# Grouped feed-forward: order of shared and routed blocks, of the routing's products, and of the weight remainders

## What is computed (the reference, cut)

```python
scores = softmax(x @ gate_w.T)                       # 16 experts
topk_w, topk_idx = top_k(scores, 4); topk_w /= sum(topk_w)
for each expert e:  y += w_e * ((silu(x @ wg_e.T) * (x @ wu_e.T)) @ wd_e.T)     # I = 176
y += (silu(x @ sg.T) * (x @ su.T)) @ sd.T            # shared, I = 352
x = x + y
```

## Time and profile before

| | |
|---|---|
| median of 3 runs | 1520.65 us (1513.06 to 1520.93) |
| the profiled execution | 1517.63 us, span 1515.8 us, mean granted TensorE clock 0.936 |
| TensorE matmul busy | 1306.7 us (86%) |
| VectorE, ScalarE, POOL busy | 1032.8, 852.6, 865.5 us (68, 56, 57%) |
| chain that ended last | PE 40%, issue 20%, POOL 18%, DVE 12%, DMA 5%, ACT 3% |
| gathers, L1041 | 94, mean 1060 ns |
| scatters, L1050 | 94, mean 1012 ns |
| raw weight loads | 36 of 608 KB |

### The profile page before, as it was taken

The page is one execution under the profiler, slowest core; times in us unless marked ns, Lnnn a source line. Parts: engine busy times, 40 slices in busy tenths (PEclk is TensorE's granted clock), DMA queues, the critical chain, the costliest instruction groups (busy, mean ns, idle before and its releaser), DMA issues.

```text
span 1515.8 us, 28468 instructions
## 1 busy us (share of the span) xinstructions
PE 1306.7 (86%) x8066; PEld 1100.9 (73%) x8066; DVE 1032.8 (68%) x2536; ACT 852.6 (56%) x2102; POOL 865.5 (57%) x760
## 2 busy tenths in 40 slices
PE   5999999999777993759899999899999989768983
PEld 3888888888767883537777777677777769667872
DVE  5676666657547544438888888788888867547544
ACT  1444444454326542238787877687787866226542
POOL 3555555531335774257877777778687721235772
PEclk8999999999869997769999999999999999779996
DMA  3000000002325336121222222222222202326335
GB/s 114 26 26 26 26 25 25 16 27 67 108 85 174 113 102 226 40 57 34 65 58 70 60 57 54 57 55 56 57 53 50 50 16 75 122 71 195 102 103 180
DMA packets 52271, 110.72 MB, mean 73 GB/s; under 512 B 11616, under 2 KB 21408, under 8 KB 51872
## 3 DMA queue, kind: packets, MB, share of 16 engines
q1 hardware_dynamic: 40992, 82.22, 18.9%
q0 software_dynamic: 9024, 24.65, 5.5%
q10 hardware_dynamic: 2112, 2.10, 0.4%
HBM read 64.11 MB, written 15.47 MB: 52 GB/s over the span
## 4 chain that ended last, share of the span: by engine, by line
PE 40%; issue 20%; POOL 18%; DVE 12%; DMA 5%; ACT 3%; POOLq 0%; SPq 0%; DVEq 0%; ACTq 0%
PE ps L1463 26%; PE ps L1618 7%; POOL pb_odd L1102 4%; POOL yt L1102 3%; DMA raw_w<-in_wx 3%; POOL rb L1087 2%; PE ps L1826 2%; POOL z L1102 2%; DVE rb L545 2%; DVE x_res L855 2%; POOL ra L1091 1%; POOL pb_low L1102 1%; DMA xg<-zbuf,gidx 1%; PE ps L1716 1%; PE ps L1550 1%
## 5 line engine op out<-in xcount | busy, mean ns | idle before, releaser
L914 DVE TENSOR_TENSOR pt_lo<-ps,pt_hi 128x512 fp32r<-128x512 f32 (+3 forms) x384 | 205.3, 549 | 52.4 <-ACT pt_hi L1382 46.2
L1463 PE MATMUL ps<-kh,qh 128*128 128x512 f32 (+3 forms) x768 | 203.1, 374 | 20.9 <-DMA qh<-qt_hi 9.0
L1382 ACT CAST pt_hi<-ps 128x512 fp32r<-128x512 f32 (+3 forms) x384 | 178.8, 482 | 56.4 <-PE ps L1826 48.5
L899 DVE TENSOR_REDUCE nmb<-ps 128x1 f32<-128x1024 f32 (+7 forms) x256 | 191.9, 750 | 27.1 <-PE ps L1463 26.0
L1463 PEld LDWEIGHTS ps<-kh,qh 128*128 128x128 f32 x768 | 131.2, 195 | 44.1 <-issue 12.8
L1463 PE MATMUL ps<-pt_hi,vst 128*128 128x512 f32 (+3 forms) x384 | 155.8, 406 | 1.6 <-DVE ra L879 1.6
L1041 POOL DMA_INDIRECT xg<-zbuf,gidx x94 | 99.6, 1060 | 58.4 <-PE ps L1688 23.0
L1463 PE MATMUL ps<-pt_lo,vst 128*128 128x512 f32 (+3 forms) x384 | 132.2, 348 | 0.0
L1179 ACT ACTIVATE pa<-sma,nmax 128x192 f32<-128x192 f32 x128 | 57.3, 449 | 129.4 <-DVE nmax L582 105.2
L1006 POOL TENSOR_TENSOR pa<-pa,rinv 128x384 f32<-128x384 f32 x64 | 52.9, 827 | 130.6 <-DVE rinv L590 130.6
L1463 PE MATMUL ps<-w_ex,gx_hi 128*128 x376 | 102.4, 355 | 18.6 <-issue 17.7
(11 more groups left out here) (223 smaller groups left out, 4206.8 us busy)
## 6 DMA issues: line engine op xcount, KB each, us to landing
raw_w<-in_wx SPq DMA_DIRECT2D x36, 608.0 KB
rb<-raw SPq DMA_DIRECT2D x192, 64.0 KB, 2.0
yg<-ybuf SPq DMA_DIRECT2D x8, 1024.0 KB, 8.0
qh<-qt_hi SPq DMA_DIRECT2D x64, 128.0 KB, 2.3
qh<-qt_lo SPq DMA_DIRECT2D x64, 128.0 KB, 2.4
wa<-in_wa SPq DMA_DIRECT2D x16, 384.0 KB, 3.0
wb<-in_wb SPq DMA_DIRECT2D x8, 384.0 KB, 3.3
wo_a<-in_wo_a SPq DMA_DIRECT2D x16, 128.0 KB, 2.0
```

Of the source, the lines that this page charges most:

```text
L899: v.tensor_reduce(nmb[:, par, i:i + 1], ps[:, b:b + 2, :].rearrange("p b k -> p (b k)")[:, 0:P * (t + 1)], AX.X, ALU.max, negate=True).the ...
L914: v.tensor_tensor(pt_lo[:, s % 3, at], ps[:, 4 + s % 2, at], pt_hi[:, s % 3, at].bitcast(F32), ALU.subtract).then_inc(sem("b_pt_lo"), 1)
L1382: s_.copy(pt_hi[:, s % 3, at], ps[:, 4 + s % 2, at]).then_inc(sem("b_pt_hi"), 1)
L1463: return t_.matmul(o, l, r, start=start, stop=stop)
```

## The change

- `ORDER`: ten shared blocks, then three times two routed and two shared ones, then the remaining routed blocks. Before: twelve, and twice two and two.
- The second logits move from step 4 to 3, the ranks from 5 to 4, and both halves of the table stand in step 7.
- VectorE: `tables` stands ahead of `experts`; `shifted` comes one step later; in the first stage the remainder of attention b's value weights moves from behind the last step into the last but one.
- ScalarE: the exponential moves behind the last block's output.
- POOL takes the remainders of weights 0 to 5 only; VectorE takes 6 and 7 too. The steps of all copies and remainders are new.

```diff
--- before.py
+++ after.py
@@ -51,12 +51,14 @@
 NBP = 48
 NSH = NT * N_SH
 NM = NSH + NB
-FRONT = 12
-ORDER = ([("s", n) for n in range(FRONT)] + [("r", 0), ("r", 1), ("s", 12), ("s", 13), ("r", 2), ("r", 3), ("s", 14), ("s", 15)] +
-         [("r", b) for b in range(4, NB)])
+FRONT = 10
+ORDER = [("s", n) for n in range(FRONT)]
+for u in range((NSH - FRONT) // 2):
+    ORDER += [("r", 2 * u), ("r", 2 * u + 1), ("s", FRONT + 2 * u), ("s", FRONT + 2 * u + 1)]
+ORDER += [("r", b) for b in range(NSH - FRONT, NB)]
 AT = {item: j for j, item in enumerate(ORDER)}
 N_W = N_SH + NE
-POOL_LO = 8
+POOL_LO = 6
 XG_RING = 4
 YB_RING = 4
 TILE_ROWS = TOPK * P + TOPK
@@ -829,15 +831,16 @@
                 step(5)
                 hot(1)
                 step(6)
+                tables()
                 experts()
-                tables()
+                step(7)
                 shifted()
-                for j in range(7, NM):
+                for j in range(8, NM):
                     step(j)
-                if s == "f":
-                    dve.wait_ge(sem("b_wv_hi"), 1)
-                    v.tensor_tensor(wvb_lo[:, :, :], wvb[:, :, :], wvb_hi[:, :, :].bitcast(F32),
-                                    ALU.subtract).then_inc(sem("b_wv_lo"), 1)
+                    if s == "f" and j == NM - 2:
+                        dve.wait_ge(sem("b_wv_hi"), 1)
+                        v.tensor_tensor(wvb_lo[:, :, :], wvb[:, :, :], wvb_hi[:, :, :].bitcast(F32),
+                                        ALU.subtract).then_inc(sem("b_wv_lo"), 1)
                 dve.wait_ge(sem(f"{s}_ex"), since(s, "ex") + 1)
                 link(v.tensor_reduce(csum[:, :], ex[:, :, :], AX.X, ALU.add))
                 link(v.reciprocal(cinv[:, :], csum[:, :]))
@@ -1310,9 +1313,6 @@
                         x_hi(ORDER[j + 2][1])
                     if j + 1 < NM:
                         silu(j + 1)
-                    if j + 1 == NM:
-                        act.wait_ge(sem(f"{s}_shifted"), since(s, "shifted") + 1)
-                        s_.activation(ex[:, :, :], ex[:, :, :], ACT.Exp).then_inc(sem(f"{s}_ex"), 1)
                     h_hi(j)
                     if j == 1:
                         norm(s, 1, ACC[before][1])
@@ -1328,6 +1328,8 @@
                         elif j == NM - 3:
                             w_hi_b(0)
                 y_out(NB - 1)
+                act.wait_ge(sem(f"{s}_shifted"), since(s, "shifted") + 1)
+                s_.activation(ex[:, :, :], ex[:, :, :], ACT.Exp).then_inc(sem(f"{s}_ex"), 1)
 
             ffn("f", "a")
 
@@ -1743,13 +1745,12 @@
                 for j in range(NM):
                     if j == 2:
                         norm(s, 1, ACC[before][1])
+                    elif j == 3:
+                        logits(s, 1)
                     elif j == 4:
-                        logits(s, 1)
-                    elif j == 5:
                         ranks()
                     elif j == 7:
                         table(0)
-                    elif j == 8:
                         table(1)
                     if j + 2 < NM and ORDER[j + 2][0] == "r":
                         turn_x(ORDER[j + 2][1])
@@ -1995,9 +1996,9 @@
 
 CB_SIZE = 2848 + 2 * P
 CF_SIZE = 282 + NBP
-ACT_HI = {0: (2,), 2: (3,), 4: (4,), 6: (5,), 8: (6,), 9: (7,), 12: (8,), 14: (9,), 16: (10,), 17: (11,),
-          19: (12,), 20: (13,), 22: (14,), 23: (15,), 25: (16,), 26: (17,)}
-DVE_LO = {13: (8,), 15: (9,), 17: (10,), 18: (11,), 20: (12,), 21: (13,), 23: (14,), 24: (15,), 26: (16,), 27: (17,)}
+ACT_HI = {0: (2,), 1: (3,), 2: (4,), 3: (5,), 5: (6,), 7: (7,), 9: (8,), 10: (9,), 12: (10,), 13: (11,), 15: (12,), 16: (13,),
+          18: (14,), 19: (15,), 22: (16,), 23: (17,)}
+DVE_LO = {7: (6,), 8: (7,), 10: (8,), 11: (9,), 13: (10,), 14: (11,), 16: (12,), 17: (13,), 19: (14,), 20: (15,), 23: (16,), 24: (17,)}
 
 FIRST_PIECES = (0, 2, 1, 3, 4, 5)
 FIRST_BANKS = (4, 5, 3, 4, 7, 5)
```

## The result

The changed kernel takes 1497.82 us (median of 4 runs, 1496.18 to 1499.85) against 1519.07 us for the kernel before on the same chip (4 runs): a ratio of 0.9867, 95% interval 0.9836 to 0.9899. The profiled execution took 1498.32 us, its span 1496.5 at a mean granted clock of 0.943 (before: 1515.8 at 0.936). The forecast was 1496, and the gain of some 21 us is clear of the noise. In the profiled execution the two stages gave more than that, and the attention between them gave some back.

What follows compares the result with a forecast made beforehand. POOL's rate from block 19's gather on was taken as the bound. Block 19 earlier by 10.8 and 10.6 us plus tails of 0.7 and 0.9 gave 23.0 us off: 1494.6 or 1497.6, forecast 1496, range 1485 to 1509 us.

Steps and rivals of the forecast that it cites:

- The 27 pairs: From block 19's gather to block 46's, POOL issues gather and scatter without rest: 69.36 us, 2.57 each, unchanged.
- Routing, 2.4 us: Before the first gather: logits and ranks one place earlier give 4.1 us, less 1.7 for early copies and TensorE's pieces.
- POOL's release, 10.2 us: Remainders of experts 6 and 7 leave POOL's queue, so the first gather follows its index at once: 10.2 us.
- Ten shared blocks first, 2.4 us each: First gather to block 19: two shared blocks now between routed ones cost 2.4 us each, 4.8 a stage.
- stream of weights: Check on expert weights up to block 19: four cycles of 9.35 us from 442 end at 479; block 19 at 493.
- Tail, 0.7 and 0.9 us: Stage ends: exponential behind the last output gives 0.9 us; the first stage gives back 0.2 for a moved value remainder.
- a tail with the drain: Stage end if the exponential's table load included a drain, 2.66 us in all: up to 2.4 us a stage.
- VectorE's remainders, charged with nothing: VectorE's two new remainders may slow POOL's gathers by 0.8 us each, 1.6 a stage at most, hidden in POOL's waits.
- B: Rival: shared blocks fill waits of the weight stretch, all lead kept, 32.7 us gained, 1485 to 1488 us; chance 0.15.
- C: Rival: weight loads become the limit, 1505 to 1509 us; sign: ScalarE's raw-weight waits exceed 15 us; chance 0.17.
- D: Rival: routing chain stays put behind ScalarE's early copies, POOL has nothing to gather, 1514 to 1521 us; chance 0.08.
- E: Rival: TensorE's clock stays low after the last weight, up to 1.8 us lost a step, up to 1545 us; chance 0.05.

Runs made afterwards that it cites:

- after_again: The changed kernel run once more with no edit; 1495.52 us.
- routing_back: The changed kernel with logits, ranks, both table products and the experts' index back in their old places; 1508.76 us.
- pool_only: The kernel before, with only POOL's remainders of experts 6 and 7 given to VectorE in steps 9 and 10; 1498.77 us.
- pool_back: The changed kernel with the remainders of experts 6 and 7 back on POOL, ahead of the gathers; 1505.81 us.
- order_back: The changed kernel with the old order of blocks, twelve shared blocks first; 1494.23 us.
- after: The changed kernel itself, with all edits to the kernel before; 1497.82 us.
- plan_back: The changed kernel with the old plan of weight copies and remainders, experts 6 and 7 still on VectorE; 1487.78 us.
- spread: The changed kernel with the copies of experts 8 to 17 one every second step, instead of two in three steps; 1487.01 us.
- exp_back: The changed kernel with the exponential and its table load back ahead of the last h_hi; 1497.05 us.
- dense: The changed kernel with the copies of experts 8 to 15 in eight steps running (9 to 16); 1504.28 us.
- spread_12: The changed kernel with one expert copied every second step and the old order, twelve shared blocks first; 1486.91 us.
- spread_late: The changed kernel with copies of experts 3 to 7 in their old steps, then one in two steps, the last in step 27; 1490.58 us.

## Why the prediction was right, and where it was not

**The total was right, and the size of the stages nearly, in part by luck:** 11.1 and 13.5 us against 11.5 and 11.5 (block 19 and tail together). Block 19's gather was forecast at 493 and came at 493.04; measured from the norm it moved by 10.2 and 12.0 us, against 10.8 and 10.6. The 27 pairs behind it took 562.40 - 493.04 = 69.36 us, to the hundredth what they took before. POOL's rate was the right bound to count with. The first gather, forecast 15.7 and 15.4 us earlier, came 13.2 and 16.7 us earlier behind the norm. The luck is in the parts. Beside POOL's 10.2 us the sum had 5.5 won by routing and tables and 4.8 lost by the order, so the rest came to little. It does come to little, but for other reasons: POOL's release brings 12.0 and 14.2 us by itself, the order costs nothing that these runs can show, and the plan of copies, which the sum charged with nothing behind the first gather, takes back what the routing wins.

**Routing, 2.4 us.** The logits start behind xt_lo as said, yet in the profiled execution TensorE's clock fell at 402.20 (granted 1.00 from 401 to 402 us, 0.60 from 402 to 403, 0.50 from 403 to 406; TensorE had been busy for 0.85 us of the one before): 18 of the 24 products start 0.21 us apart instead of 0.11, and lg comes at 406.22, 11.6 us behind the norm as before (11.4). In after_again lg is 9.8 us behind it, and 9.7 to 10.3 in seven of the other eight runs with the new place: 1.6 us earlier than before, against the 1.7 predicted. ScalarE did stand in step 2, 4.0 us until 406.21, a little less than the 406.8 to 408.8 forecast. From the norm to the index routing_back takes 37.7 and 38.5 us, the changed kernel 33.5 to 34.3 and 33.2 to 33.3. That is 3.4 to 5.2 us, against 5.5. But an earlier choice hardly reached the index. VectorE has the choice (chosen) 15.7 us behind the norm in the changed kernel and 11.9 in after_again, 3.8 earlier, and the index follows at 34.3 and 33.5, only 0.8 earlier. So the 4.1 us for logits and ranks were mis-sized; what the two moves brought apart from the joined table halves (3.1 predicted) was not tried.

**POOL's release, 10.2 us.** Right at the gather (0.9 us of wait are left). But as a share of the gain it was sized too low: I took it as two thirds of a lead of which part would be given back, and pool_only shows it to be worth 12.0 and 14.2 us a stage by itself, while pool_back shows only 4 and 5 us for it when the other edits are in place. The place in the prediction that failed is the addition of leads as if they were independent. In the kernel before, TensorE stands for 8 us and comes back at a granted clock of 0.50:

```profile
445.00:450.00 5.00, 2.30 (x9) 2.23 (x10) 0.42 (x1) 0.38 (x1) 3.79 (x4) 0.50 0.63 215
```

The release removes both (in pool_only the clock is 0.95 or more from 430 us on), and the rest of the stretch also shrinks from 60.1 to 56.5 us. That the clock is what shrinks it is not shown.

**Ten shared blocks first, 2.4 us each.** Its total was near: first gather to block 19 took 63.0 us against 64.9. Its cause was wrong: this is the second place that failed. With the old order (order_back) that stretch took 60.8 and 63.4 us, against 63.0 and 64.8 (after, after_again) in the first stage and 63.3 and 63.1 in the second, so at most 2.2 to 4.0 us in one stage and nothing in the other. What both stages pay for is the plan of copies, which the sum charged with nothing there: plan_back is 3.4 and 1.8 us shorter than the changed kernel, spread 6.0 and 3.3. I had checked the stream of weights and it ran on time, the last copy at 478.57 against 479. What I did not price is that this copy stands in step 23, with steps 12 to 23 stretched by ScalarE's waits. An early copy is no gain if the steps behind it have still to be run.

**Tail, 0.7 and 0.9 us.** 14.2 against 15.0, and 12.9 against 14.4 before; exp_back gives some 0.4 to 0.8 us of the second to the exponential. In the first stage the moved remainder of the value weights seems to help, where the prediction charged 0.2 us: in the kernel before it runs from 585.53 to 586.75, and the scatter of 586.19 beside it takes 1.40 us instead of 0.97; pool_only shows the same (574.37, and 1.40 at 575.02), and exp_back, with the remainder moved, has 0.97 at that place. The 2.4 us that the prediction gives for a tail with the drain does not come out of its terms: 0.9 and the 1.38 between 2.66 and 1.28 are 2.3.

**VectorE's remainders, charged with nothing.** The two new ones start at 431.05 and 437.12, and the gathers beside them took 1.48 us at 431.54 and 1.85 at 437.23, against 0.97, as the earlier trace rows said; 1.78 and 1.77 at 459.19 and 471.28 stand beside remainders that VectorE had before. POOL waited for TensorE before or soon after each (0.46 to 1.86 us), so I take them as hidden. In spread, where POOL has less to wait for, such a gather is on its path (that of 486.83 took 1.41 us), a cost of 0.4 us.

**The rivals.** B (all of the lead kept) is near what pool_only does, and what the whole change does not. C's sign, ScalarE's waits over 15 us a stage, stayed just short: 12.6 us in eight waits, against 7.5 in five before. dense shows C's mechanism in earnest. D and E did not come: the index moved, and the stretch behind block 19 ran as before.

## What to carry to other kernels

Before adding up leads of several edits, ask which of them alone removes the idle gap; here handing the remainders of two experts from POOL's queue to VectorE's did nearly all of it, and the further edits with it summed to about nothing. A prefetch plan tied to loop steps has a rate: measure the stream's time per item (4.0 to 4.4 us) and divide by the time that a step needs (2.2 to 2.6 us), and plan no denser than that, or the in-order engine that fetches makes every step wait. And compare stages from a marker of their own in the trace: an untouched stretch here moved by up to 9 us from one execution to the next, nearly half of the gain.

## What was unexpected

**A cast of 32 columns waited for POOL.** VectorE's CAST of 128x32 takes 0.18 us; after it took 2.13 us at 407.64, and ended at 409.77, as did POOL's remainder of expert 4:

```profile
407.49 2.24 POOL L1033 TENSOR_TENSOR w_ex<-raw_w,w_ex 128x960 fp32r<-128x960 f32 x1 [2.04 <-ACT w_ex L1264]
```

In pool_back it took 2.04 us from 407.40 beside the same instruction, 407.16 to 409.40; in routing_back 1.28 us from 407.97 beside that of 406.99 to 409.21. Where the cast came first (407.65 against 406.23 in spread) it took 0.18. VectorE's TENSOR_TENSOR on 128x256 right behind it took 0.42 to 0.43 us in all of these. The Trainium skill (SBUF — State Buffer, Who interferes with whom) says that a cast may take the port pair shared with GpSimd for itself, and that whoever comes second is blocked, not slowed; the rows agree. The same section's inference that descriptor writing stays free of a VectorE instruction with two SBUF inputs is not what the rows look like: 1.85 against 0.97 us at 437.23. They can't refute it either, since the index column that a gather needs (gidx) lies in SBUF too, and a read of it may be what was held.

**The same 2 us fell on another instruction where the cast escaped.** In after_again:

```profile
411.31 2.68 DVE L718 TENSOR_TENSOR hit<-hit,spos 128x512 f32<-128x512 f32 x1
```

```profile
411.23 2.21 POOL L1033 TENSOR_TENSOR w_ex<-raw_w,w_ex 128x960 fp32r<-128x960 f32 x1
```

After has 0.69 us for the first of these in its first stage and 2.69 in its second; exp_back, order_back, spread, dense and spread_12 have 2.67 to 2.70 in both. plan_back and spread_late, with the late copies of experts 3 to 7, have 0.69 and a cast of 0.18, yet their index is no more than 0.5 us ahead of after_again's (33.1 and 33.5, 33.1 and 32.9 us behind the norm, against 33.5 and 33.2). So these 2 us hardly reach the index.

**A lower clock did not decide it.** spread's granted clock from 430 to 440 us was no better than that of the changed kernel:

```profile
430.00:435.00 5.00, 3.30 (x15) 2.93 (x13) 2.58 (x7) 1.63 (x4) 3.95 (x4) 0.50 0.43 120
435.00:440.00 5.00, 5.00 (x28) 4.87 (x27) 4.00 (x10) 2.37 (x6) 2.59 (x2) 0.66 0.52 154
```

It reached block 19 first all the same. Why attention varies between 695.4 and 704.7 us was not tried, and stays open.
